# A quantization block's scale and reciprocal: from two rows of a tile to neighbouring words

## What is computed

```python
def fp4_quant_dequant(x):
    xb = x.reshape(shape[:-1] + (shape[-1] // 16, 16))
    scale = jnp.maximum(jnp.max(jnp.abs(xb), axis=-1, keepdims=True) / 6.0, 1e-12)
    xn = xb / scale
    idx = jnp.searchsorted(_MID, jnp.abs(xn))
    return (_GRID[idx] * jnp.sign(xn) * scale).reshape(shape)

gate = fp4_linear(xn, w_gate)      # 512 -> 1408, both operands quantized
y = fp4_linear(xn, w_up)
return fp4_linear(jax.nn.silu(gate) * y, w_down)
```

## Time and profile before

| | |
|---|---|
| median of 3 runs | 3094.61 us (3094.44 to 3095.01) |
| span of the profiled execution | 3092.0 us |
| what lies around that span, against the median | 2.6 us |
| PE busy | 2991.3 us, 97% |
| DVE busy | 2177.3 us, 70% |
| POOL busy | 1519.8 us, 49% |
| ACT busy | 1146.4 us, 37% |
| mean granted clock of PE | 0.998 of full speed |

### The profile page before, as it was taken

How to read it: one execution, slowest core, us unless ns; L and a number is a source line. 1 busy time by engine, 2 the same in 40 slices (tenths; PEclk the granted TensorE clock), 3 DMA queues, 4 the chain that set the end, 5 groups by cost and what they waited for, 6 DMA issues and landing times.

```text
span 3092.0 us, 43985 instructions
## 1 busy us (share of the span) xinstructions
PE 2991.3 (97%) x14573; PEld 2417.7 (78%) x14573; DVE 2177.3 (70%) x4451; ACT 1146.4 (37%) x1934; POOL 1519.8 (49%) x1417
## 2 busy tenths in 40 slices
PE   5799999999999999999999899999999999999999
PEld 3678888888887777777777788788888888888887
DVE  7798898887877677777777676776665656565622
ACT  5445656644453343433433343222222222222220
POOL 7556666665555555554555235423444434353513
PEclk9999999999999999999999999999999999999999
DMA  4133343346766666666643458777777676768541
GB/s 126 48 86 93 118 118 107 97 133 180 191 175 171 162 168 163 154 162 172 166 120 99 126 134 203 170 178 205 203 179 205 174 214 168 206 165 218 150 127 48
DMA packets 965425, 469.89 MB, mean 152 GB/s; under 512 B 688080, under 2 KB 816336, under 8 KB 962640
## 3 DMA queue, kind: packets, MB, share of 16 engines
q1 hardware_dynamic: 965200, 467.08, 58.0%
HBM read 330.06 MB, written 136.87 MB: 151 GB/s over the span
## 4 chain that ended last, share of the span: by engine, by line
PE 66%; DVE 18%; issue 5%; POOL 5%; DMA 2%; ACT 2%; SPq 1%; DVEq 0%; POOLq 0%; ACTq 0%
PE bank L1225 16%; PE bank L1203 15%; PE bank L1029 14%; PE bank L1051 7%; PE bank L1152 4%; PE bank L1168 4%; DVE qs L1349 3%; POOL qa L2124 2%; DVE qa L1366 2%; PE bank L1092 2%; DVE qs L1360 2%; DVE qa L1322 2%; POOL qa L2118 1%; DVE qb L1374 1%; PE bank L999 1%
## 5 line engine op out<-in xcount | busy, mean ns | idle before, releaser
L1029 PE MATMUL bank<-XT,Wu 128*128 128x512 f32 (+1 forms) x2148 | 515.5, 389 | 16.1 <-DVE sg L1314 15.8
L1029 PE MATMUL bank<-XT,Wg 128*128 128x512 f32 (+1 forms) x2148 | 522.8, 392 | 7.3 <-DVE Wd L1381 7.3
L1051 PE MATMUL bank<-Wd,HT 128*128 128x512 f32 x2112 | 515.5, 393 | 6.6 <-POOL HT L2132 5.3
L1029 PEld LDWEIGHTS bank<-XT,Wu 128*128 128x128 f32 x2148 | 400.9, 190 | 106.7 <-issue 25.9
L2124 POOL TENSOR_TENSOR qa<-qb,qs 128x512 f32<-128x512 f32 (+2 forms) x277 | 308.5, 1114 | 342.3 <-DVE qb L1374 337.8
L1051 PEld LDWEIGHTS bank<-Wd,HT 128*128 128x128 f32 x2112 | 391.8, 188 | 106.2 <-issue 15.4
L1029 PEld LDWEIGHTS bank<-XT,Wg 128*128 128x128 f32 x2148 | 397.4, 189 | 95.9 <-DVE Wd L1381 9.4
L1225 PE MATMUL bank<-Wp,G 128*128 128x512 f32 x1536 | 388.4, 389 | 5.1 <-POOL G L2249 5.1
L1203 PE MATMUL bank<-HC,Wp 128*128 128x512 f32 x1440 | 361.7, 389 | 1.7 <-POOL WH L2242 1.7
L2132 POOL TENSOR_TENSOR HT<-qb,HT 128x512 fp32r<-128x512 f32 (+1 forms) x179 | 229.9, 1284 | 242.2 <-ACT HT L1817 242.0
L1225 PEld LDWEIGHTS bank<-Wp,G 128*128 128x128 f32 x1536 | 288.1, 188 | 66.1 <-POOL G L2249 6.3
(11 more groups left out here) (199 smaller groups left out, 4543.4 us busy)
## 6 DMA issues: line engine op xcount, KB each, us to landing
Wp<-r_A SPq DMA_DIRECT2D x336, 256.0 KB, 3.5
px<-in_L_attn_x_dram SPq DMA_DIRECT2D x128, 256.0 KB, 3.3
xin<-in_L_attn_x_dram SPq DMA_DIRECT2D x128, 256.0 KB, 3.4
sT<-r_K SPq DMA_DIRECT2D x128, 256.0 KB, 4.2
r_Z<-xin SPq DMA_DIRECT2D x64, 256.0 KB, 2.4
r_U<-ub SPq DMA_DIRECT2D x16, 1024.0 KB, 6.7
sU<-r_U SPq DMA_DIRECT2D x32, 512.0 KB, 5.1
r_Y<-sY SPq DMA_DIRECT2D x16, 1024.0 KB, 5.6
```

The costliest lines, as they stand in the source:

```text
L1029: ins = e.matmul(bk[:, 0:n], W[wh][:, k, :], inputs(xh, w, k), start=(k == 0 and p_ == 0), stop=(k == KD - 1 and p_ == 2))
L1051: ins = e.matmul(DNB[t % 4][:], HT[hh][:, w % 2, a * P:(a + 1) * P], Wd[wh][:, f, :], start=(w == first(n) and p_ == 0), stop=(w == last(n ...
```

## The change

The two last dimensions of `qs` are exchanged. Before, the 32 scales of a job lay one after the other (step 4 bytes) and its 32 reciprocals after them. After, each scale is followed by its reciprocal, so that both are reached with a step of 8 bytes from block to block. The tile has the same size and place, the same instructions are issued in the same order with the same waits, and each instruction handles as many elements as before.

```diff
-        qs = sbt(actx, "qs", [P, 4, 2, 32])
+        qs = sbt(actx, "qs", [P, 4, 32, 2])
...
             def biggest(m):
-                s_ = qs[:, m % 4, 0, 0:n // 16]
+                s_ = qs[:, m % 4, 0:n // 16, 0]
...
             def inverse(m):
-                e.reciprocal(qs[:, m % 4, 1, 0:nb], qs[:, m % 4, 0, 0:nb]).then_inc(s_rc, 1)
+                e.reciprocal(qs[:, m % 4, 0:nb, 1], qs[:, m % 4, 0:nb, 0]).then_inc(s_rc, 1)
...
             def front(m):
-                s_ = qs[:, m % 4, 0, 0:job_width(m) // 16]
+                s_ = qs[:, m % 4, 0:job_width(m) // 16, 0]
...
             def weight_inverse(m):
-                    r_ = qs[:, m % 4, 1, 0:job_width(m) // 16]
+                    r_ = qs[:, m % 4, 0:job_width(m) // 16, 1]
...
             def scale(m):
-                s_ = qs[:, m % 4, 0, 0:job_width(m) // 16]
+                s_ = qs[:, m % 4, 0:job_width(m) // 16, 0]
...
             def scaled(m):
-                    r_ = qs[:, m % 4, 1, 0:n // 16]
+                    r_ = qs[:, m % 4, 0:n // 16, 1]
...
-                e.tensor_tensor(blk(qa[:, m % 4, 0:n]), blk(job_in(m)), bc(qs[:, m % 4, 1, 0:n // 16], n // 16),
+                e.tensor_tensor(blk(qa[:, m % 4, 0:n]), blk(job_in(m)), bc(qs[:, m % 4, 0:n // 16, 1], n // 16),
                                 ALU.mult).then_inc(s_pa, 1)
...
             def dequant(m):
-                e.tensor_tensor(blk(qa[:, m % 4, 0:n]), blk(qb[:, m % 2, 0:n]), bc(qs[:, m % 4, 0, 0:n // 16], n // 16),
+                e.tensor_tensor(blk(qa[:, m % 4, 0:n]), blk(qb[:, m % 2, 0:n]), bc(qs[:, m % 4, 0:n // 16, 0], n // 16),
                                 ALU.mult).then_inc(s_ph, 1)
```

## The result

The changed kernel takes 3098.98 us at the median of 21 runs (3096.08 to 3101.41), the kernel before 3093.73 in as many (3090.23 to 3096.63): 5.25 us more, a ratio of 1.0017 with a 95% interval of 1.0011 to 1.0022. The forecast was 3096.5 us and "same" within 0.2%. The loss is real and 2.6 times the one forecast. At 0.17% it lies just inside the bound of 0.2%, and its interval reaches past it.

The account below looks back on a forecast made before the run. From 200 to 700 us DVE, with POOL's multiplies, was taken to set the pace, balanced with PE within about 1%. POOL's 1.4 and DVE's 0.6 us made +2.0, 3096.5 us; the 8-in-10 range was 3089 to 3104.

Parts of the forecast that it names:

- POOL's multiplies: Lines 2118 and 2124: the reciprocal and scale multiplies each take 14 ns more, bounds -14 to 40; 1.4 us in all.
- Or 75 instructions: POOL multiplies on the chain from 200 to 700 us, from 54.5 and 25 us of chain time; 100 overall.
- DVE's tensor_scalar: Line 1360, 244 times: 8 ns more where not held by POOL, bounds 0 and 33; 0.6 us in all.
- never held that way: Line 1417 on DVE, said never to wait for POOL: 164 to 168 ns at 8 bytes, so no price shown.
- The estimate of 23 to 46 ns: Line 1360 longer by this much, by a Trainium skill page's table; the sum would be 2 to 4 us higher.
- Reduce, reciprocal, scale, ACT: Lines 1349, 1354, 2106 and 1805: 0 ns each, strided accesses hidden or off the pace; upper bounds given, no gain.
- No operation feels the step: Rival for the whole kernel: neither the 14 ns nor the 8 ns arises, 3094.6 us; 30%.
- The slower one: Rival: POOL's two multiplies cost as much as ordinary products, 230 ns more each, about 28 us, 3122 us; 10%.
- Its deciding point: For the slower rival: from 62 ns more per POOL multiply the change passes the bound of 0.2%, 6.2 us.
- The faster one: Rival: line 1360 is no longer held by POOL, 190 instead of 434 ns, 3086 us; 7%.
- together 494 of 500: PE's needed time from 200 to 700 us, 481.5 plus 12.1 us, capping the faster rival's gain there at 6 us.
- the likeliest case: Total time the same within 0.2%, given 0.82, against 0.07 for faster and 0.11 for slower.

## Why the prediction came out as it did

**POOL's multiplies: the right operations, both factors too small.** "So 16 x 0.9 = 14 ns more per instruction": measured 23 (1064 to 1087), inside the bounds of -14 to +40. That it is these reads that cost, and in which direction, was read well from the difference between broadcast and ordinary products; the price was not. Against a step of 4, that price asks for 14, 29, 43 and 86 ns at 8, 12, 16 and 28 bytes, and 23, 30, 43 and 42 were measured. It fits at two steps of four, so the price is not one per 8 bytes passed, and what it is stays open.

**How many count: the term that was furthest off.** "Or 75 instructions" from 200 to 700: measured, the windows grew by 46.7 ns, two multiplies each. That is as if all 118 of the 59 hidden-layer jobs counted there and those of the side jobs did not, though no run tells which ones count. The shares of the chain left some out. One way in which that happens can be seen. In the changed kernel's timeline, POOL's line 2118 runs to 306.97, line 1412 is held until 306.99, and line 1417 then until 308.23, until POOL's 2137, which follows 2118 on POOL, has ended at 308.21:

```profile
305.88 1.09 POOL L2118 TENSOR_TENSOR qa<-qa,qs 128x512 f32<-128x512 f32 x1 [0.56 <-DVE qs L1354]
...
306.60 0.39 DVE L1412 TENSOR_SCALAR rtmp<-mv 128x8 f32<-128x8 f32 x1
...
307.02 1.21 DVE L1417 SCALAR_TENSOR_TENSOR rtmp<-rtmp,mv 128x8 f32<-128x8 f32 x1
```

The chain of waits books such time on DVE, since DVE's record is open. All nine of line 1412's SBUF form went from 360 to 366 ns to 376 to 394, by the 20 ns or so that line 2118 lasts longer:

```profile
L1412 DVE TENSOR_SCALAR rtmp<-mv x9: 376/383/394, 131.3 to 648.4; 128x8 f32<-128x8 f32 x6, 128x4 f32<-128x4 f32 x3
```

With 118 in place of 75 and 23 in place of 14 ns, the 200 to 700 us stretch costs 2.7 us instead of 1.05, and 80 windows 3.7. The head, the first windows and the last ones bring it to 6.0 us at window 178 in this pair of profiles; the medians differ by 5.25. What lies outside windows 10 to 90, 1.5 to 2.3 us, is not told apart from chance by single profiles.

**DVE's tensor_scalar.** "I take 8 ns": measured 0. Its minimum stayed at 181 ns and the run with strided DVE accesses alone lengthened no window (0.2 ns). Line 1417 had been the right witness for the pace, but "never held that way" misread its row: its maximum is 1211 ns, and three of the nine are held by POOL's line 2137, as in the timeline just shown. The estimate of 23 to 46 ns from the Trainium skill's page "Vector Engine (DVE) Microarchitecture Reference", section 5.2, whose table has no step of 2 words, does not show in any run here at 32 elements and 8 bytes. The lines of 16 bytes in "Advanced Engine Details and Errata", SBUF Cachelines, of the Trainium skill fit what was measured. That the hold would stay, read from line 1412, was right: 739 ns at most after, 734 before.

**Reduce, reciprocal, scale, ACT.** Taken at 0: reduce 686 and reciprocal 353 as before. The scale on POOL took 3 ns more, 0.1 us over 33, and line 1805 on ACT 233 ns in place of 229, 0.1 us over 29.

**The rivals.** "No operation feels the step" fell with POOL's rows. The slower one (POOL at the price of an ordinary product, 3122 us) did not come: 23 ns, not 230. Its deciding point, 62 ns per multiply for 0.2%, was set with 100 multiplies; with two per window in some 100 windows and the head it lies near 27 (6.2 us x 23/5.25), so the change at 23 stopped just short of it, and that it did is luck. The faster one did not come by the change, as line 1412 foretold; built on purpose, it was worth 12.4 us and not 9. The cap "together 494 of 500" was wrong: it took the 64 small matmuls at their recorded 12.1 us, while two of them pass in 0.14 us, some 4.5 us in all, which leaves 14 us and not 6; about 10 of them were gained.

**The range** of 3089 to 3104 held 3098.98, and the ratio ended within 0.2%, as the likeliest case had it, though its interval reaches past that bound. The sum itself was low by more than half.

## What to carry to other kernels

A broadcast operand on POOL is cheaper packed than interleaved: here the interleaving cost 2% of each multiply, and the loop, which passes through POOL twice a window, paid two such prices in each. To count how often an operation is on the pace-setting loop, do not add its shares of the chain: instructions held by it on another engine hide some; compare the length of a period after and before. And look for short instructions with a second, much longer duration: moving such an operand to an idle PSUM bank gained more than twice what the change lost.

## What was not expected of the hardware

POOL's multiply by a broadcast operand depends on the step between blocks: 1041, 1062, 1085, 1092, 1105 and 1104 ns at 0, 4, 8, 12, 16 and 28 bytes. A DVE tensor_scalar of 32 elements with source and destination at 8 bytes has the minimum of the packed one (181 ns) and is held by POOL as before, and from PSUM it takes 191 ns and is not held (194 at most in 134). Beside a PE busy share of 99% stood room for 2% more matmuls, since a matmul recorded with 391 ns is followed by the next after 227.
